# Four normalisations without TensorE's products of zeros

## The reference

```
x = x + attention(gn(x))      # layer 0
x = x + prelu_scan(gn(x))     # layer 1
x = x + attention(gn(x))      # layer 2
x = x + relu_scan(gn(x))      # layer 3
```

## Time and profile before

| | us |
|---|---|
| median of 3 runs | 274.9 |
| lowest and highest | 274.88, 275.43 |
| profiled execution, its time | 274.79 |
| span of its profile, first to last instruction | 273.0 |
| PE busy, PEld busy | 262.0, 225.0 |
| DVE, ACT, POOL busy | 167.7, 99.1, 64.9 |

### The profile page before, as it was taken

One profiled execution on the slowest core, in us unless ns is written; L12 is line 12 of the kernel. 1 busy time (PEld: TensorE's weight loads), 2 busy tenths in 40 slices (PEclk: granted clock), 3 DMA queues, 4 the chain that ended last, 5 costly groups with the idle time before them and its releaser, 6 DMA issues.

```text
span 273.0 us, 11058 instructions
## 1 busy us (share of the span) xinstructions
PE 262.0 (96%) x4536; PEld 225.0 (82%) x4539; DVE 167.7 (61%) x634; ACT 99.1 (36%) x229; POOL 64.9 (24%) x94
## 2 busy tenths in 40 slices
PE   6989999999979999999999999999998999999996
PEld 1668888888479999999984888788885799999995
DVE  2695454555667777777778863563668455555553
ACT  2144544545653342433320655638339200000000
POOL 0109200004222233333331040000040432333442
DMA  7990000000000000000000000000000000002122
GB/s 232 413 371 7 0 0 2 1 0 0 0 5 4 0 0 0 0 0 0 0 1 0 0 0 2 1 1 0 2 0 0 2 0 0 0 19 70 66 77 77
DMA packets 4479, 9.25 MB, mean 34 GB/s; under 512 B 624, under 2 KB 3056, under 8 KB 3952
## 3 DMA queue, kind: packets, MB, share of 16 engines
q1 hardware_dynamic: 4176, 8.53, 8.4%
q10 hardware_dynamic: 288, 0.52, 0.6%
HBM read 6.96 MB, written 2.10 MB: 33 GB/s over the span
## 4 chain that ended last, share of the span: by engine, by line
PE 82%; DVE 8%; ACT 4%; issue 2%; DMA 2%; POOL 1%; POOLq 0%; ACTq 0%; DVEq 0%
PE banks L377 44%; PE banks L298 18%; PE banks L354 7%; PE banks L310 5%; DVE st L543 3%; PE banks L317 2%; ACT xn L455 2%; PE banks L270 2%; PE banks L329 2%; DMA x<-in_x 2%; PE banks L345 1%; POOL rstd L830 1%; ACT rel L468 1%; PE banks L286 1%; PE banks L279 1%
## 5 line engine op out<-in xcount | busy, mean ns | idle before, releaser
L377 PE MATMUL banks<-state,wc 128*64 128x64 f32 x3840 | 121.5, 224 | 1.5 <-DVE state L717 1.5
L377 PEld LDWEIGHTS banks<-state,wc 128*64 128x64 f32 x3840 | 116.9, 138 | 6.3 <-issue 1.6
L298 PE MATMUL banks<-xn,w 128*128 128x256 f32 x256 | 60.9, 383 | 0.0
L298 PEld LDWEIGHTS banks<-xn,w 128*128 128x128 f32 x256 | 46.4, 190 | 6.5 <-issue 1.3
L695 DVE SCALAR_TENSOR_TENSOR state<-banks,negb,inb 128x64 f32<-128x64 f32 x116 | 29.2, 281 | 25.4 <-PE banks L377 23.8
L830 POOL TENSOR_TENSOR rstd<-gvar,mhalf 128x4 f32<-128x4 f32 (+1 forms) x8 | 14.6, 1827 | 121.9 <-DVE gvar L576 121.9
L712 DVE SCALAR_TENSOR_TENSOR sloped<-banks,par,share 128x64 f32<-128x64 f32 x116 | 27.6, 280 | 16.0 <-PE banks L377 16.0
L354 PE MATMUL banks<-probT,xnT 128*128 128x256 f32 x128 | 29.5, 381 | 0.8 <-ACT rel L468 0.8
L354 PEld LDWEIGHTS banks<-probT,xnT 128*128 128x128 f32 x128 | 24.2, 190 | 4.8 <-ACT rel L468 1.6
L717 DVE SCALAR_TENSOR_TENSOR state<-sloped,bent,banks 128x64 f32<-128x64 f32 x112 | 26.1, 276 | 0.0
L498 ACT COPY banks<-inb 128x256 f32 (+1 forms) x29 | 10.9, 376 | 38.3 <-DVE state L717 36.2
(11 more groups left out here) (76 smaller groups left out, 210.8 us busy)
## 6 DMA issues: line engine op xcount, KB each, us to landing
w<-in_w SPq DMA_DIRECT2D x2, 1024.0 KB, 9.9
wc<-in_wc SPq DMA_DIRECT2D x2, 1024.0 KB, 13.2
result<-xh SPq DMA_DIRECT2D x15, 128.0 KB, 1.8
x<-in_x SPq DMA_DIRECT2D x3, 512.0 KB, 8.3
x<-in_x ACTq DMA_DIRECT2D x1, 256.0 KB, 4.6
x<-in_x SPq DMA_DIRECT2D x1, 256.0 KB, 4.4
w<-in_w ACTq DMA_DIRECT2D x1, 256.0 KB, 5.0
w<-in_w SPq DMA_DIRECT2D x1, 256.0 KB, 11.3
```

Source lines behind the costliest of these rows:

```text
L298: mm = nc.tensor.matmul(bank[2 + m // 2][:, m % 2 * POS:(m % 2 + 1) * POS], w3[l][:, k, m * P:(m + 1) * P], xn_s[:, k], start=(k == 0), st ...
L377: mm = nc.tensor.matmul(bank[K * h + m][c:c + TILE, 0:COLS], wc[l][:, k, m * P + c:m * P + c + TILE], state[:, h, k], start=first and not ...
```

## The change

`keep_warm`, its three tables and its three calls in `critical_norm` go. Nothing else differs: the other engines have the same programs. The block of zeros is still cleared, since `clear_banks` and an activation read it.

```diff
-WARM_STATS = [9, 6, 12, 6]
-WARM_MEANS = [3, 3, 3, 3]
-WARM_VARIANCES = [11, 11, 9, 11]
...
-            def keep_warm(count, b=7):
-                for _ in range(count):
-                    nc.tensor.matmul(bank[b], zeros[:, 0:P], zeros[:], start=True, stop=True)
...
             def critical_norm(l, r):
-                keep_warm(WARM_STATS[l], 3 if l == 2 else 7)
                 group_means(l, r)
-                keep_warm(WARM_MEANS[l])
                 group_variances(l, r)
-                keep_warm(WARM_VARIANCES[l])
```

## The result

The changed kernel takes 281.45 us (median of 4 runs, 280.15 to 282.79) against 275.16 for the kernel before (4 runs). The ratio is 1.0229, interval 1.0203 to 1.0255. In absolute terms that is 6.3 us slower; the forecast was 280.7 in a range of 276.8 to 285.5. The profiled execution took 281.51 us.

A forecast was written before the change was run, and what follows sets the result against it. PE was taken to bound the kernel, with 82% of what sets the end. Terms 1.15 + 0.6 + 2.0 + 1.7 + 0.45 = 5.9 us on the profiled 274.79 gave 280.7 us, range 276.8 to 285.5.

The forecast's parts named there:

- layer 0, image 0 and two group products: Start of layer 0: PE at the lower clock delays the first image 0.85 us and group products 0.3; 1.15 us (0.35 to 2.25).
- scan 1, first step: First step of scan 1 takes 3.6 to 4.0 us instead of 2.09, so the second starts late; 0.6 us (0.2 to 1.5).
- layer 2, image 0: First image of layer 2 begins at the lower clock with everything on PE; loses 2.0 us (1.45 to 2.6).
- scan 3: Last scan begins at the lower clock, losing 2.1 us less 0.4 for its earlier start; 1.7 us (1.1 to 2.55).
- later group products: Group products of the three later normalisations, some at the lower clock; 0.45 us (0 to 0.9).
- The level falls in all three stretches: Ahead of scan 1, layer 2 and scan 3, stretches of 5.3, 6.3 and 5.5 us each drop PE's clock.
- The time at the lower level, T: How long PE works at the lower clock before it gets the upper; taken as 4.5 us (3.4 to 5.7).
- The pace: At the lower clock, layer 0's first eight projection instructions take 3.4 us, a scan's first step 3.6 to 4.0 us.
- The gain from an empty queue in layer 0: Layer 0's first real product, ready about 10.4 but started at 10.61, no longer waits behind zeros; gain 0.15 us.
- A fall in some stretches only: Rival: the clock falls only in some of the three later stretches, giving 277 to 280 us, middle 278.7; chance 0.2.
- a later rise than with zeros: Rival: at the four stage starts real work lifts the clock 2 us later than zeros did, giving 284.7 us; chance 0.12.
- a gain from the queue: Rival: no clock loss at any of four places, only 0.3 to 0.65 us gained from queue, giving 274.3 us; chance 0.03.

The follow-up runs named there:

- single experiments: Kernel before with the zeros of one normalisation left out at a time: ratios 1.0023 (layer 0), 1.0047 (layer 1), 1.0098 (layer 2), 1.0056 (layer 3).

## Why the prediction was right

The mechanism was right at each of its four places, and the sum (5.9 us against 6.7 by the spans and 6.3 by the medians) is a little short. By its terms, from the two chains:

| term | predicted | measured in the profile |
|---|---|---|
| layer 0, image 0 and two group products | 1.15 | 1.62 (20.85 - 19.23) |
| scan 1, first step | 0.6 | 0.7 (81.73 - 79.19 = 2.54, less 1.62 and 0.2) |
| layer 2, image 0 | 2.0 | 2.2 |
| scan 3 | 1.7 | 2.05 (2.43 longer, 0.38 earlier) |
| later group products | 0.45 | 0.2 |

The term of layer 2 is its third block of L290 at 160.84 against 156.18 before, less the 2.48 us by which DVE's statistics ahead of it already started later (145.72 against 143.24), with no group product in it that was slow.

*The level falls in all three stretches.* This was the step without a row behind it, and it held: three dips in the granted clock. The Trainium skill, "TensorE: Matmul & The Clock Gate", Part 1, which says that idling brings the lower rate back, agrees with this trace (1.00 to 0.50 at 73.7 us, PE's last real product at 71.4).

*The time at the lower level, T.* Forecast 4.5 us (3.4 to 5.7) after the stage's first product; measured 4.7, 3.4, 4.5 and 5.6. The bounds from one rise held for all four, which is luck in part. Where zeros and group products were all that PE had done, as where T came from, the lists of clocks of six other runs put the rise 2.9 to 9.3 us after the product at 1.20. Without layer 1's zeros alone it came 2.7 us after the start of scan 1, without layer 3's alone 2.8 after that of scan 3, and with only the first group everywhere 5.9 after it. What the chain loses depends on how much of the low stretch is over when the stage begins, and T hides that. What decides where in a stretch it falls, no run here tells. Scan 3 had the longest, which is why its term was mis-sized: 1.7 for 2.05.

*The pace.* The eight projection instructions took 3.75 us, 3.4 forecast. By the timeline the transposes start at 14.65, 3.55 us after the first of the eight, so about 0.2 of the 0.35 us is the last product's end, under which the next work has begun; the rest was not taken apart. The scan's first step took 3.65, in the forecast's 3.6 to 4.0; its end delayed DVE as described.

*The group products.* Each costs 0.2 us at the lower level: 0.57 and 0.60 in place of 0.39. In layer 0 both did, in scan 1 the second, and in layers 2 and 3 neither, because the fall came behind them. PE's pauses around them were longer than the 1.7 us of the prediction: up to 2.40 us (ahead of layer 2's group means). The timeline of the changed kernel:

```profile
6.73 0.57 PE L271 MATMUL banks<-st,gavg 128*128 128x8 f32 x2 [6.73 <-DVE st L532]
8.16 0.60 PE L278 MATMUL banks<-vadd,gavg 128*128 128x8 f32 x2 [0.86 <-DVE vadd L558]
11.10 3.75 PE L302 MATMUL banks<-xn,w 128*128 128x256 f32 x8 [2.34 <-DVE xn L576]
```

*The gain from an empty queue in layer 0*, 0.15 us, does not exist. The prediction took a quarter of DVE's 1.38 us as the time of the first tile. The chain after has the first product 0.56 us behind the start of L576 (10.54 to 11.10), the same as before (10.05 to 10.61); the first tile takes longer than a quarter. Without that 0.15, and with 0.2 for each group product, layer 0's term would have been 1.4.

*The rivals.* A fall in some stretches only did not happen; the level came up in both scans; a later rise than with zeros was not seen (T within its bounds). In layer 2 the rise at 155.6 fell among the transposes, and the low stretch there was as long (6.8 us) as in the scans, which have none. The Trainium skill, same page, Part 4, on the full clock not engaging for transposes, is not borne out here by float32 ones: eight take 1.29 us across the rise and 0.87 at the upper level. In the run with only the first group of zeros, where the rise came as the first image's transposes ended, they take 1.79 us by the timeline, and 1.04 in the kernel before. The rival on the other side, a gain from the queue, is measured apart as nothing (0.9999, to within 0.13%).

## What to carry to other kernels

Products that nobody needs can pay: 87 of them, in stretches where TensorE only waited, are worth 6.3 us of 275. In this kernel the same number with an eighth of the columns is worth nothing, one group at either end recovers about a quarter, and half of them in every place a little more than half. When judging such a stretch, count what comes after it at the lower pace (here 0.6 to 2.7 us for each stage, by the single experiments) and look for slack there: the two stages in which PE had a wait for another engine to give up, image 0 of layer 0 and scan 1, lost least (scan 1 and scan 3 are closer than their intervals by the single experiments, 1.3 and 1.5 us). And a profile is one execution: that of the kernel without layer 1's zeros showed 3.4 us of lower level, where seven of ten runs had 10.2. The clock of every run is worth reading before a stage's cost is taken from one trace. And read the pace of the first instructions, not only the granted clock.

## What the runs showed of the hardware

- The granted clock reads 1.00 from the start of every trace, while the first products run at half pace (eight 256-column float32 instructions in 3.75 us in place of 1.9). Only what comes from the first rise on is in the record.
- The first rise moves from run to run under the same first instructions. With nine or twelve zeros from 1.20 us on and the group means, it came at 4.1, 5.1, 5.2, 6.3, 10.2 and 10.5 us in six profiles, by the traces' lists of clocks.
- The low stretches that both began and ended within a profile lasted 3.4 or 6.8 us, as near as the windows tell: 6.8 three times in the changed kernel, 3.4 three times with half the zeros, both in the runs with one group.
- A loss can come after work has begun: with only the first group, scan 1 ran fast until 77.7 us and was slow for 3.4 us then. With half the zeros layer 2's image began at 149.26 and the level fell at 149.4.
- Float32 products at half pace: the scans' 64 instructions take 3.65 us in place of 2.09 (1.75 times), the images' 256-column ones twice as long.
